# Tail of an attention layer on one core: row maxima and scores ahead, second PSUM banks for output and weighted values, four rows of outputs and residuals

## What is computed

```python
h = jnp.maximum(_layernorm(x, axis=-1), 0.0)
q, k, v = split_heads(h @ Wq), split_heads(h @ Wk), split_heads(h @ Wv)   # 4 heads of 64
sim = jnp.einsum('bhid,bhjd->bhij', q, k) * scale
sim = jnp.where(adjacency_mask[:, None, :, :], sim, neg)
attn = jax.nn.softmax(sim, axis=-1)
out = jnp.einsum('bhij,bhjd->bhid', attn, v)        # heads merged to 256 columns
x = x + out @ Wo + bo
```

## Time and profile before

| | |
|---|---|
| median of 3 runs | 2672.29 us (2670.97 to 2674.83) |
| the profiled execution, its own time | 2663.97 us |
| its span, first to last instruction | 2662.2 us |
| mean granted TensorE clock | 0.992 |
| busy: TensorE, VectorE, ScalarE, GpSimd | 97%, 75%, 66%, 53% of the span |

### The profile page before, as it was taken

One profiled execution on the slowest core, in us unless ns is written; L12 is line 12 of the kernel. 1 busy time (PEld: TensorE's weight loads), 2 busy tenths in 40 slices (PEclk: granted clock), 3 DMA queues, 4 the chain that ended last, 5 costly groups with the idle time before them and its releaser, 6 DMA issues. The chain is left out here.

```text
span 2662.2 us, 62523 instructions
## 1 busy us (share of the span) xinstructions
PE 2592.3 (97%) x20886; PEld 1395.0 (52%) x20886; DVE 1984.7 (75%) x6361; ACT 1748.8 (66%) x5020; POOL 1401.7 (53%) x2790
## 2 busy tenths in 40 slices
PE   6999999999999999999999999987999999999998
PEld 3455555555555555555555555554555555555554
DVE  5477778777877777778777777785777777777765
ACT  3566666666666666666666666675777777777774
POOL 4255545545554555455545554544565556556552
PEclk9999999999999999999999999998999999999998
DMA  5367766776677666667766776577777777878763
GB/s 141 61 140 157 144 137 132 146 154 129 143 152 144 131 137 146 151 130 137 150 147 129 137 149 147 130 163 180 163 169 165 159 167 160 173 155 174 159 144 92
DMA packets 945488, 387.43 MB, mean 146 GB/s; under 512 B 857616, under 2 KB 859152, under 8 KB 945168
## 3 DMA queue, kind: packets, MB, share of 16 engines
q1 hardware_dynamic: 945168, 383.44, 68.2%
HBM read 114.86 MB, written 67.11 MB: 68 GB/s over the span
## 5 line engine op out<-in xcount | busy, mean ns | idle before, releaser
L549 ACT ACTIVATE probs<-probs,negmax 128x128 f32<-128x128 f32 x1024 | 398.3, 390 | 454.8 <-DVE negmax L124 454.8
L462 POOL TENSOR_TENSOR o_sb<-o_sb,xres 128x512 f32<-128x512 f32 x128 | 162.7, 1271 | 504.2 <-DVE o_sb L738 501.0
L166 PE MATMUL l_ps_pj<-hT,room 128*128 128x512 f16 x1488 | 345.3, 382 | 1.2 <-ACT room L1339 1.2
L166 PE MATMUL ps_pj<-wm_hi,hT 128*128 128x512 f16 x1024 | 326.1, 380 | 10.8 <-DVE wm_lo L760 6.8
L166 PE MATMUL ps_pj<-wv_hi,hT 128*128 128x512 f16 x1024 | 326.4, 380 | 0.0
L166 PE MATMUL ps_pj<-hT,wk_hi 128*128 128x512 f16 x1024 | 305.8, 380 | 0.0
L166 PE MATMUL ps_pj<-hT,wq_hi 128*128 128x512 f16 x1024 | 304.5, 379 | 0.0
L1353 ACT ACTIVATE l_probs<-l_probs,l_negmax 128x128 f32<-128x128 f32 x512 | 199.1, 390 | 159.4 <-DVE l_negmax L124 159.4
L1290 POOL TENSOR_TENSOR l_h<-l_h 128x512 f16<-128x512 f32 x120 | 139.4, 1162 | 265.6 <-ACT l_h L1332 162.3
L124 DVE CUSTOM_DVE_ANT_0 probs<-ps_sc,mask 128x128 f32<-128x128 f32 x1024 | 235.3, 285 | 47.8 <-PE ps_sc L983 47.2
L720 DVE SCALAR_TENSOR_TENSOR c<-cprobs,c 128x512 f16<-128x512 f32 x256 | 184.5, 721 | 79.6 <-ACT c L556 79.2
(11 more groups left out here) (171 smaller groups left out, 6158.6 us busy)
## 6 DMA issues: line engine op xcount, KB each, us to landing
xg<-in_x SPq DMA_DIRECT2D x128, 256.0 KB, 3.3
xres<-in_x SPq DMA_DIRECT2D x128, 256.0 KB, 3.0
x_scratch<-o_sb SPq DMA_DIRECT2D x128, 256.0 KB, 2.4
out<-o_sb SPq DMA_DIRECT2D x128, 256.0 KB, 3.3
l_ring<-x_scratch SPq DMA_DIRECT2D x124, 256.0 KB, 3.2
mask_u<-in_adj SPq DMA_DIRECT2D x64, 64.0 KB, 2.6
cpT<-c SPq DMA_TRANSPOSE x256, 3.2
xg<-x_scratch SPq DMA_DIRECT2D x12, 256.0 KB, 3.7
```

What stands on the lines that cost most here:

```text
L166: last = pe.matmul(out, a(kt), b(kt), start=(n == 0), stop=(n == 3 * kts - 1))
L462: nc.gpsimd.tensor_tensor(o_sb[:, j % 2], o_sb[:, j % 2], xres[:, j % 2], ALU.add).then_inc(res_done, 1)
L549: last = nc.scalar.activation(probs[:, i], probs[:, i], ACT.Exp, bias=negmax[:, u % 2, i:i + 1], scale=-1.0, accum_out=zsum[:, u % 4, hh:h ...
```

## The change

In the body of layer 1 (iterations 0 to 123) the order stays. Iterations 124 to 126 become a loop of their own on TensorE, VectorE and ScalarE, with scores ahead of project_out on TensorE, row_max(n+2) right behind normalise(n+1) on VectorE, and aT_high behind p_high on ScalarE. ps_av and ps_o become two banks each, so that their waits look one graph further back. xres and a new tile out_sb have four rows, with semaphores of their own for the stores. GpSimd's wait is for residual i−4.

```diff
-        xres = sb("xres", [P, 2, D])
+        xres = sb("xres", [P, 4, D])
+        out_sb = sb("out_sb", [P, 4, D])
-        ps_av, ps_o = bank("ps_av"), bank("ps_o")
+        ps_av = [bank("ps_av0"), bank("ps_av1")]
+        ps_o = [bank("ps_o0"), bank("ps_o1")]
...
+        out_stored = [sem(f"out_stored{n}") for n in range(4)]
...
-                sp.dma_start(out[i], o_sb[:, i % 2]).then_inc(o_stored[i % 2], 16)
+                sp.dma_start(out[i], out_sb[:, i % 4]).then_inc(out_stored[i % 4], 16)
...
-            for n in range(2):
-                sp.wait_ge(o_stored[n], stored0 + 16 * (B // 2))
+            for n in range(4):
+                sp.wait_ge(out_stored[n], 16 * (B // 4))
...
-                pool.wait_ge(out_done, count(i - 1))
-                nc.gpsimd.tensor_tensor(xres[:, i % 2], row(i), bo_rows[:], ALU.add).then_inc(res_ready, 1)
+                if i >= 4:
+                    pool.wait_ge(out_done, count(i - 3))
+                nc.gpsimd.tensor_tensor(xres[:, i % 4], row(i), bo_rows[:], ALU.add).then_inc(res_ready, 1)
...
+            for n in range(B - QUAD, B - 1):
+                exps(n + 1)
+                p_high(n + 1)
+                aT_high(n - 2)
+            for i in range(B - 3, B):
+                aT_high(i)
...
-                dve.wait_ge(o_stored[n % 2], stored0 + 16 * (n // 2))
-                nc.vector.scalar_tensor_tensor(o_sb[:, n % 2], ps_o[:], unscale["o"], xres[:, n % 2], ALU.mult,
+                if n >= 4:
+                    dve.wait_ge(out_stored[n % 4], 16 * (n // 4))
+                nc.vector.scalar_tensor_tensor(out_sb[:, n % 4], ps_o[n % 2][:], unscale["o"], xres[:, n % 4], ALU.mult,
...
-            add_residual(B - 4)
-            aT_low(B - 2)
-            add_residual(B - 3)
-            aT_low(B - 1)
+            row_max(B - 3)
+            for n in range(B - QUAD, B - 1):
+                add_residual(n - 4)
+                normalise(n + 1)
+                if n + 2 < B:
+                    row_max(n + 2)
+                p_low(n + 1)
+                aT_low(n - 2)
+            for i in range(B - 5, B - 2):
+                add_residual(i)
+                aT_low(i + 2)
             add_residual(B - 2)
             add_residual(B - 1)
...
-                pe.wait_ge(alo_done, count(n))
+                pe.wait_ge(alo_done, count(n - 1))
...
-                pe.wait_ge(out_done, count(n))
+                pe.wait_ge(out_done, count(n - 1))
...
+            for n in range(B - QUAD, B - 1):
+                scores(n + 1)
+                project_out(n - 4)
+                weigh_values(n - 2)
+            project_out(B - 5)
+            weigh_values(B - 3)
             project_out(B - 4)
             weigh_values(B - 2)
             project_out(B - 3)
```

More of the change, by code:

```diff
@@ L1364, in aT_high @@
                 act.wait_ge(o_ready, count(n - 1))
-                nc.scalar.activation(aT_hi[:, n % 2], ps_av[:, 0:PAIRS1 * P].rearrange("p (k n) -> p k n", k=PAIRS1), ACT.Copy,
+                nc.scalar.activation(aT_hi[:, n % 2], ps_av[n % 2][:, 0:PAIRS1 * P].rearrange("p (k n) -> p k n", k=PAIRS1), ACT.Copy,
                                      scale=1.0 / F16_SCALE).then_inc(ahi_done, 1)
@@ L1373, in _ @@
             h_high(MADE + 1)
-            for n in range(B):
-                if n + QUAD < B:
-                    qk_copy(n + QUAD)
+            for n in range(B - QUAD):
+                qk_copy(n + QUAD)
                 if n + 10 < B:
@@ L1379, in _ @@
                     h_high(n + 10)
[L1380 to L1383, removed]
+                exps(n + 1)
+                v_high(n + QUAD)
                 if n >= 2:
                     aT_high(n - 2)
[L1386 to L1389, removed]
+                p_high(n + 1)
+            for n in range(B - QUAD, B - 1):
+                exps(n + 1)
+                p_high(n + 1)
+                aT_high(n - 2)
+            for i in range(B - 3, B):
+                aT_high(i)
         @block.vector
@@ L1427, in aT_low @@
                 dve.wait_ge(ahi_done, count(n + 1))
-                nc.vector.scalar_tensor_tensor(aT_lo[:, n % 2], ps_av[:, 0:PAIRS1 * P].rearrange("p (k n) -> p k n", k=PAIRS1),
+                nc.vector.scalar_tensor_tensor(aT_lo[:, n % 2], ps_av[n % 2][:, 0:PAIRS1 * P].rearrange("p (k n) -> p k n", k=PAIRS1),
                                                1.0 / F16_SCALE, aT_hi[:, n % 2], ALU.mult, ALU.subtract).then_inc(alo_done, 1)
@@ L1442, in _ @@
                 stats(i)
-            for n in range(B):
+            for n in range(B - QUAD):
                 if n >= 4:
                     add_residual(n - 4)
-                if n + 1 < B:
-                    row_max(n + 1)
+                row_max(n + 1)
                 if n + 15 < B:
                     stats(n + 15)
[L1450 to L1453, removed]
+                normalise(n + 1)
+                v_low(n + QUAD)
                 if n >= 2:
                     aT_low(n - 2)
-                if n + 1 < B:
-                    p_low(n + 1)
-            add_residual(B - 4)
-            aT_low(B - 2)
-            add_residual(B - 3)
-            aT_low(B - 1)
+                p_low(n + 1)
+            row_max(B - 3)
+            for n in range(B - QUAD, B - 1):
+                add_residual(n - 4)
+                normalise(n + 1)
+                if n + 2 < B:
+                    row_max(n + 2)
+                p_low(n + 1)
+                aT_low(n - 2)
+            for i in range(B - 5, B - 2):
+                add_residual(i)
+                aT_low(i + 2)
             add_residual(B - 2)
@@ L1514, in weigh_values @@
                             hh = 2 * pr + b
-                            mm = nc.tensor.matmul(ps_av[DH * b:DH * b + DH, pr * P:(pr + 1) * P],
+                            mm = nc.tensor.matmul(ps_av[n % 2][DH * b:DH * b + DH, pr * P:(pr + 1) * P],
                                                   v_part[:, g % 2, j, hh * DH:(hh + 1) * DH],
@@ L1521, in project_out @@
                 pe.wait_ge(alo_done, count(n + 1))
-                pe.wait_ge(out_done, count(n))
-                split_products(nc.tensor, ps_o[:], lambda k: aT_hi[:, n % 2, k, :], lambda k: aT_lo[:, n % 2, k, :],
+                pe.wait_ge(out_done, count(n - 1))
+                split_products(nc.tensor, ps_o[n % 2][:], lambda k: aT_hi[:, n % 2, k, :], lambda k: aT_lo[:, n % 2, k, :],
                                lambda k: w_hi["o"][:, k, :], lambda k: w_lo["o"][:, k, :], PAIRS1).then_inc(o_ready, 1)
             scores(0)
-            for n in range(B):
-                if n + QUAD < B:
-                    project_qk(n + QUAD)
+            for n in range(B - QUAD):
+                project_qk(n + QUAD)
                 if n >= 4:
                     project_out(n - 4)
[L1532 to L1535, removed]
+                scores(n + 1)
+                project_v(n + QUAD)
                 if n >= 2:
                     weigh_values(n - 2)
+            for n in range(B - QUAD, B - 1):
+                scores(n + 1)
+                project_out(n - 4)
+                weigh_values(n - 2)
+            project_out(B - 5)
+            weigh_values(B - 3)
             project_out(B - 4)
```

## The result

| | before | after |
|---|---|---|
| median (range), 7 runs each | 2669.70 us (2667.63 to 2674.83) | 2662.43 us (2658.97 to 2665.13) |
| the profiled execution, its span | 2662.2 us | 2657.2 us |
| scores(124) starts, the tail's beginning | 2625.04 | 2626.44 |
| last residual starts | 2658.95 | 2653.93 |
| tail, from the one to the other | 33.91 us | 27.49 us |

The change makes the kernel faster: ratio 0.9969, 95% interval 0.9960 to 0.9978. The measured 7.3 us are smaller than the 10.15 forecast; that the predicted time of 2662.1 fits to 0.3 us is luck: the kernel before, run more often, came out 2.6 us lower than the median that the prediction started from, and so made up for most of the gain that is missing.

The account below looks back on a forecast made before the run. TensorE bounds the body; after the last projections no engine is full and a serial row does. Span 2662.2 − 9.55 (tail) − 0.6 (body) = 2652.05 us; median 2672.29 − 10.15 = 2662.1 us, range 2659.8 to 2669.3.

Parts of the forecast that it names:

- Row maximum ahead: VectorE in the tail: row_max(125) goes ahead of residual 120, from 2631.45 to 2630.79; last transpose issued 4.76 us earlier.
- The ring: Tail's repeating cycle of row maximum, exponentials, reciprocal and normalise: 3.46 us between row maxima, where rows took 5.51.
- The queues passed: SyncE's order and GpSimd's xres adds in the tail: nothing late, three 1.27 us adds off the path.
- Rival C: GpSimd's xres add, released earlier, contends with VectorE's work in the body: slower, 2676.5 us; chance 0.05.
- The landing: Last transpose in the tail: median landing of 3.1 us assumed; the longest, 5.2, would be 1.7 us late.
- The drain: End of the tail, project_out(124) to the last residual: two banks and four rows let TensorE run back to back, gaining 4.79 us.
- Scores first: TensorE in the tail: scores(n+1) ahead of project_out(n−4), worth nothing by itself, only cover for the row cycle.
- Body: Looser waits in the body of layer 1: between 0 and 1.1 us of TensorE idleness, taken as 0.6.
- Rival A: TensorE's clock falls and the drain runs at half clock: 3.8 us gained with the body, 2668.5 us; chance 0.24.
- bank rule: TensorE's clock: cycling through PSUM banks leaves micro-idles that make it swing; by it the two banks bring 2668.5 us.

Follow-up runs that it names:

- Buffers alone: Second banks, four rows and looser waits as in the change, but with the old tail loops, against the kernel before: ratio 0.9973, tail 30.46 us.
- order alone: The kernel before, with one bank each and two rows, given only the new loops for the tail: ratio 0.9988, tail 31.24 us.

## Why the prediction was right, and where it wasn't

It was right in kind: faster, by the tail, with the body giving a little. Step by step, the times counted from scores(124), which started at 2625.04 before:

- *Row maximum ahead.* row_max(125) was forecast at 5.75 us and came at 5.75. The ring was forecast at 3.46 us and took 3.58 where nothing disturbed it (row 126, and both rows with eight rows of xres). The step that failed was in "The queues passed": "three 1.27 us adds ahead of need, off the path". The adds are off the path by their result, but not by their place. They follow the residual, the residual had been moved in front of normalise, and normalise took 0.93 us more in two rows. The ring's own 0.12 comes twice as well: the row maximum waits until normalise is done, so it starts 2635.77 − 2635.05 = 0.72 us after normalise's start, where the prediction took 0.61, the distance to an instruction that overlaps normalise. So the transpose of 127 came 2.13 us late: 19.76 for 17.63. Rival C named this contention and priced it for the body, where VectorE's waits do cover it (TensorE idle 0 of 760 us); I never asked what it would cost in the tail, where normalise is the path.
- *The landing.* "I take the median, as this stretch moves few bytes." The bytes were few, but one transpose in the tail meets the instruction packet, and in the changed kernel it was the last. Its term was 4.4 in place of 3.1, of which 1.0 us reached the end. 2.13 + 1.0 is the difference between 9.55 and 6.42.
- *The drain.* Otherwise as computed: no wait for a residual or a store, and from project_out(126) to the last residual 2653.93 − 2651.19 = 2.74 us by the chain, forecast 1.29 + 1.49 = 2.78. Buffers alone give 3.45 us, with a late landing and the clock at half; the forecast for this part was 4.79.
- *Scores first* was said to be cover, not gain; the order of TensorE was not tried apart from that of VectorE, so this stays argued.
- *Body.* Forecast 0.6 of at most 1.1; about all of it came: the kernels with four or eight rows show 0 to 0.3 us of idleness of TensorE between 1860 and 2620, those with two rows 1.1 to 1.4.
- *Rival A* came true in part and cost the changed kernel nothing, which is the case it didn't have: a low clock matters only where TensorE is on the path. With buffers alone it is there. By the bank rule of the Trainium skill ("TensorE: Matmul & The Clock Gate", A second HAM failure mode) the second banks should have brought the low clock; measured, in the tail it was low for 17 us (before) and 6.8 us in two stretches (order alone) without them, for 3.4 us (the change) and 10.2 us in two stretches (buffers alone) with them, and with eight rows of xres and the same banks it never fell. The banks don't decide it.
- The total: tail 6.4 and body 1.1 make 7.5, measured 7.3 by the medians and 8.3 by the ratio.

## What to carry to other kernels

When a step is moved in one engine's order, look at what is triggered by its end on other engines: that work moves with it, and it may land beside an instruction that it slows. A contention that the body hides has to be priced again where the same instruction is the critical path. And in a stretch with little slack a single late landing can reach the end: nine of the eleven tails here had one, in three it was the last transpose, and in the changed kernel 1.0 of its 1.3 us reached the end. So its largest value belongs in the sum's range, not its median alone.

## What the runs showed of the hardware

- VectorE's product of two SBUF tensors (128x512, 0.69 us alone) and GpSimd's add (1.27 us alone) hold each other up for an instruction at a time: the product took 1.62 us beside one add, 1.73 beside two, the second of which took 1.59. The low half, also with two SBUF inputs, took 0.79 for 0.69 where it met the end of such an add. The residual and the row maximum, which read one operand from PSUM, ran beside such adds at their usual 0.75 and 0.29 us. The Trainium skill ("GPSIMD Engine Reference", Specifications) has the rule that VectorE's instructions with two SBUF inputs contend with GpSimd; the runs agree and add the size.
- A 16 KB packet of the instruction queue in the middle of a DMA transpose went with a landing of 4.4 to 5.0 us for 3.1, in nine of nine cases in the tails, and in the bodies with a median of 4.8 us over 73 cases (a correlation, not tried by an edit).
- The granted clock fell to 0.50 in the tail of the kernel before, where the longest idle stretch of TensorE until then was 1.65 us. It stayed at 1.00 in the tail of the kernel with eight rows, where the longest was 1.66 us.
